# How many steps of a superstep have a fixed place: one instead of two, in a graph network that builds its adjacency matrix by one-hot products

## The reference: what is computed

```python
    def _sage_conv(x, src, dst, W_l, b_l, W_r):
        msg = x[src]
        summed = jax.ops.segment_sum(msg, dst, num_segments=N_NODES)
        cnt = jax.ops.segment_sum(jnp.ones((src.shape[0],), x.dtype), dst, num_segments=N_NODES)
        aggr = summed / jnp.maximum(cnt, 1.0)[:, None]
        return aggr @ W_l + b_l + x @ W_r
...
    for l in range(L):
        agg = jax.ops.segment_sum(h[src], dst, num_segments=N) / deg
...
edge_index = jnp.stack([src, dst])
x = _layernorm(x + _L0_gnn_ref(x, edge_index, ...))
x = _layernorm(x + _L1_gnn_ref(x, edge_index, ...))
```

## Time and profile before

| | |
|---|---|
| median of 3 runs | 2031.82 us (2031.15 to 2037.95) |
| the profiled execution | 2040.89 us, of it 2039.1 us in the span |
| loop that builds A | 92 to 399 us of the span |
| PE, PEld busy over the span | 1772.0 us (87%), 1376.1 us (67%) |
| DVE, ACT, POOL busy over the span | 892.9, 829.7, 619.0 us |
| mean granted clock of TensorE | 0.907 |

### The profile page before, as it was taken

One profiled execution on the slowest core, in us unless ns is written; L12 is line 12 of the kernel. 1 busy time (PEld: TensorE's weight loads), 2 busy tenths in 40 slices (PEclk: granted clock), 3 DMA queues, 4 the chain that ended last, 5 costly groups with the idle time before them and its releaser, 6 DMA issues.

```text
span 2039.1 us, 30707 instructions
## 1 busy us (share of the span) xinstructions
PE 1772.0 (87%) x9747; PEld 1376.1 (67%) x9748; DVE 892.9 (44%) x2593; ACT 829.7 (41%) x1404; POOL 619.0 (30%) x593
## 2 busy tenths in 40 slices
PE   3856666589999998999979998999979998999974
PEld 2545555445566654888868877888868777888864
DVE  6589999834344335533321113433321113433324
ACT  6156666634322222333326563333336663333321
POOL 1044444300000033444430231544430221644430
PEclk9866666689999999999999998999989997999986
DMA  6970000034566783354448551454458541544441
GB/s 145 341 265 0 0 0 0 24 128 173 197 204 222 244 312 123 74 114 74 71 73 283 196 192 44 83 111 72 68 107 284 184 165 43 96 68 74 74 114 51
DMA packets 162537, 259.54 MB, mean 127 GB/s; under 512 B 27776, under 2 KB 136043, under 8 KB 162424
## 3 DMA queue, kind: packets, MB, share of 16 engines
q1 hardware_dynamic: 125960, 206.09, 31.5%
q0 software_dynamic: 36464, 51.98, 14.5%
HBM read 149.08 MB, written 108.94 MB: 127 GB/s over the span
## 4 chain that ended last, share of the span: by engine, by line
PE 76%; DVE 12%; issue 5%; ACT 3%; DMA 2%; DVEq 1%; SPq 1%; POOL 0%; ACTq 0%; POOLq 0%
PE psum L1685 17%; PE psum L1696 16%; PE psum L1507 14%; PE psum L1594 13%; DVE arena L764 7%; PE psum L1651 2%; PE psum L1487 2%; PE psum L1674 2%; PE psum L1422 2%; PE psum L1454 2%; PE psum L1452 1%; PE psum L1645 1%; PE psum L1718 1%; DVEq L764 1%; PE psum L1478 1%
## 5 line engine op out<-in xcount | busy, mean ns | idle before, releaser
L669 POOL DMA_INDIRECT h_rows<-arena,idx x192 | 312.9, 1629 | 420.5 <-DVE arena L1115 374.7
L1359 ACT ACTIVATE arena<-psum,b1c 128x256 f32<-128x256 f32 x384 | 181.8, 473 | 462.5 <-PE psum L1685 462.5
L1685 PE MATMUL psum<-arena 128*128 128x256 f32 x1536 | 360.6, 389 | 6.7 <-ACT arena L1356 6.7
L1696 PE MATMUL psum<-arena 128*128 x1536 | 347.4, 379 | 0.0
L1685 PEld LDWEIGHTS psum<-arena 128*128 128x128 f32 x1536 | 281.1, 193 | 70.9 <-ACT arena L1359 18.7
L1507 PE MATMUL psum<-arena 128*128 128x384 bf16 (+1 forms) x1875 | 316.9, 326 | 0.5 <-ACT arena L1243 0.2
L1696 PEld LDWEIGHTS psum<-arena 128*128 128x128 f32 x1536 | 284.6, 190 | 34.8
L764 DVE TENSOR_TENSOR arena<-arena 125x1200 bf16<-125x1200 bf16 (+1 forms) x300 | 282.4, 1008 | 20.4 <-PE psum L1454 19.5
L1507 PEld LDWEIGHTS psum<-arena 128*128 128x128 bf16 x1875 | 181.5, 98 | 125.7 <-ACT arena L1246 3.2
L644 POOL DMA_INDIRECT xs_d<-arena,pos x150 | 146.3, 976 | 390.4 <-DVEq L946 348.4
L1113 DVE TENSOR_TENSOR arena<-psum,arena 128x256 f32<-128x256 f32 x192 | 80.9, 421 | 378.2 <-PE psum L1696 377.0
(11 more groups left out here) (252 smaller groups left out, 1751.2 us busy)
## 6 DMA issues: line engine op xcount, KB each, us to landing
arena<-adj_d SPq DMA_DIRECT2D x54, 800.0 KB, 4.5
ring<-adj_d SPq DMA_DIRECT2D x46, 800.0 KB, 4.5
xs_d<-zrow SPq DMA_DIRECT2D x8, 3432.0 KB, 27.3
arena<-xs_d SPq DMA_DIRECT2D x96, 264.0 KB, 2.8
adj_d<-arena SPq DMA_DIRECT2D x25, 800.0 KB, 4.4
h_rows<-zrow SPq DMA_DIRECT2D x1, 8192.0 KB, 39.3
h_new<-h_rows SPq DMA_DIRECT2D x12, 640.0 KB, 8.0
arena<-h_rows SPq DMA_DIRECT2D x10, 640.0 KB, 6.7
```

The lines of the kernel that those rows point to most:

```text
L669: pool.indirect_dma_start(h_rows, bass.IndirectOffsetOnAxis(ap=idx[:, j % 2, h:h + 1], axis=0), ybuf[:, j % 2, h], None, compute_op=ALU.ad ...
L1359: act.activation(hid[:, j % 2, f], psum[:, 5 + f % 2, 0:M], ACT.Relu, bias=b1c[:, bass.ds(at_b1[j % LOAD] + f, 1)]).then_inc(b_hidf, 1)
L1685: mm = pe.matmul(psum[:, 5 + f % 2, 0:M], w1s[:, j % 2, f // 2, kt, f % 2 * P:(f % 2 + 1) * P], xsT[:, j % 2, kt], start=(kt == 0), stop=( ...
L1696: mm = pe.matmul(psum[:, h, 0:H], hid[:, j % 2, f, h * P:(h + 1) * P], w1f[:, bass.ds(at_w2 + f * H, H)], start=(f == 0), stop=(f == FT - 1))
```

## The change

NST goes from 2 to 1. Only step z = 0 has a fixed place; step z = 1 gets its place from a register like the other six. So `ohe` holds one step of each superstep with 200 columns (it was two with 300), `oh2` holds seven steps of each (it was six), `w_rel` has seven numbers for a superstep, and the keys are split accordingly. The count of matmuls stays. The diff, whole but for the file's head:

```diff
-NST = 2
+NST = 1
 EC = (NST + 1) * WC
...
         oh2 = carve([NOH, B16 // G * (G - NST) // 2, WC, 2], BF16, CE)
-        ohe = carve([2, B16 // G, EC, 2], BF16, CE)
+        ohe = carve([2, B16 // G // 2, EC, 2], BF16, CE)
...
-            pool.iota(iota_e[:, :, :], [[1, EC], [-WC, 2]], base=-WC, ...).then_inc(s_const, 1)
+            pool.iota(iota_e[:, :, :], [[1, EC], [0, 2]], base=-WC, ...).then_inc(s_const, 1)
...
                             if z < NST:
                                 cols = (z + 2) * WC
-                                pe.matmul(bank[:, 0:cols], oh1[:, q, n, :, z % 2], ohe[:, q % 2, g, 0:cols, z], start=(z == 0), stop=False, skip_group_check=True)
+                                pe.matmul(bank[:, 0:cols], oh1[:, q, n, :, z % 2], ohe[:, q % 2, g // 2, 0:cols, g % 2], start=(z == 0), stop=False, skip_group_check=True)
                                 continue
                             mm = pe.matmul(bank[:, bass.ds(rel[(q % 2 * k + g) * (G - NST) + z - NST], WC)], oh1[:, q, n, :, z % 2],
-                                           oh2[:, q, (g * (G - NST) + z - NST) // 2, :, z % 2], start=False, stop=(z == G - 1), skip_group_check=True)
+                                           oh2[:, q, (g * (G - NST) + z - NST) // 2, :, (g * (G - NST) + z - NST) % 2], start=False, stop=(z == G - 1), skip_group_check=True)
```

More of the change, by code:

```diff
@@ L590, in _ @@
             pool.iota(iota2[:, :, :], [[1, P], [0, 2]], base=0, channel_multiplier=0, allow_small_or_imprecise_dtypes=True).then_inc(s_const, 1)
-            pool.iota(iota_e[:, :, :], [[1, EC], [-WC, 2]], base=-WC, channel_multiplier=0, allow_small_or_imprecise_dtypes=True).then_inc(s_const, 1)
+            pool.iota(iota_e[:, :, :], [[1, EC], [0, 2]], base=-WC, channel_multiplier=0, allow_small_or_imprecise_dtypes=True).then_inc(s_const, 1)
             pool.wait_ge(s_zero, 3)
```

## The result

The changed kernel takes 2071.54 us (median of 4 runs, 2068.98 to 2077.69), the kernel before 2034.88 us (4 runs, 2031.15 to 2040.63). The ratio is 1.0186, with a 95% interval of 1.0154 to 1.0217: 38 us slower by the ratio, 37 by the medians. The forecast was 36.5.

A forecast was written before the change was run, and what follows sets the result against it. TensorE's sequencer was taken to bound the loop: 50 half turns x (0.27 read + 0.44 moved step) = 35.5, plus 1 for early half turns, is 36.5 us; 2031.82 + 36.5 = 2068 us, range 2054 to 2077.

The forecast's parts named there:

- The bound: Loop that builds A: TensorE's sequencer sets the half turn of 5.914 us; VectorE, though 96% busy, follows.
- The register read: L1435 in the loop: 28 registers instead of 24 cost 0.27 us more in each half turn, on the path.
- The moved step: Step z = 1 in every superstep, placed by a register instead of fixed: 0.11 us net, 0.44 us a half turn.
- the bank's wait: Wait instruction in TensorE's superstep: taken as two thirds of the 0.11 us it shares with three fixed pairs.
- The early half turns: First seven half turns, beside the writing of zeros: slow register reads lengthen with the count, taken as 1 us.
- Nothing outside the loop: Before the loop, tables change shape at 0, plus or minus 0.2 us; later stages are shifted and otherwise alike.
- VectorE bounds the loop: Rival in the loop: less compare work makes each batch 0.29 us shorter, 29 us off, 2003 us; chance 0.07.
- The cheap issue: Rival in the loop: added issue costs half or partly falls into slack; 24.5 us slower, 2056 us; chance 0.12.
- The array as the limit: Rival variant in the loop: 200 columns fewer a superstep take 43 us off, 1989 us; within the chance of 0.07.
- The bank's release as the pace: Rival at L1446: TensorE waits for ScalarE's L1206, which absorbs the added issue; about 2032 us, no change; chance 0.03.
- The loop's end: Sign in the profile of the changed kernel: the loop runs from 92 to about 435 us.

The follow-up runs named there:

- e1: Kernel before, with the register read at L1435 taking 28 registers instead of 24, the four more unused: half turn 6.171 us, ratio to before 1.012.
- e3: Kernel before, with VectorE's leading one-hots in the loop 200 columns wide instead of 300: half turn 5.914 us, ratio to before 1.003.
- e4: Changed kernel, with one more VectorE compare of 360 elements in each batch: half turn 6.672 us, ratio to the kernel before 1.017.
- e7: Changed kernel without TensorE's waits for oh1 and oh2, keeping that for ohe: half turn 6.413 us, ratio to the kernel before 1.016.
- e2: Changed kernel, with the register read at L1435 taking 24 registers instead of 28: half turn 6.416 us, ratio to the kernel before 1.014.
- e9: Kernel before, unchanged, run again on chip 10: half turn 5.914 us, first to last read 304.2 us, ratio to before 0.996.
- e10: Changed kernel, run again on chip 10: half turn 6.673 us, first to last read 341.9 us, ratio to the kernel before 1.012.

## Why the prediction was right

*The bound.* Shown. The argument was that the batch's one-hots are ready 2.7 and 1.6 us before they are used. A read that is 0.257 us longer makes the half turn 0.257 longer (e1), 0.20 us less of compare in a batch changes nothing (e3), 0.34 us more changes nothing in the changed kernel (e4), and a wait instruction less in each batch gives back 0.259 us in a half turn there (e7).

*The register read.* Forecast 0.27 us for four registers, measured 0.257: 12.9 of 13.5 us. The slope from ScalarE's 8 to TensorE's 24 registers, 67 ns each, nearly held at 28 (64 ns).

*The moved step.* Taken at 0.11 us for each superstep, with bounds of 0.087 and 0.122; measured 0.126 (e2), just over the upper bound. This is the term that the sum had too small. The address instructions of L1454 start 0.124 us apart (median) in both kernels; so a step placed by a register costs the sequencer about what was measured, and the fixed matmul that it replaces nothing that can be told from it. The two thirds that the prediction gave to the bank's wait were a guess, and the pair's 0.012 us with them. The sum became 50 x 0.502 = 25.1 us instead of 22. The Trainium skill's price for an issued matmul ("TensorE: Matmul & The Clock Gate", section "Wait — 56ns, not 53.3ns?", about 62 ns where hardware decode is off) doesn't fit here: by it the net price would be 0.06 us. The same section says that with hardware decode on a matmul goes to the engine without the sequencer's microcode, and with that the measurement agrees; no run here shows how the decode was set.

*The early half turns.* I took 1 us for reads that are slow beside the writing of zeros. From e9 to e10 the first nine half turns grew by 7.3 us, of which 9 x 0.759 = 6.8 is the plain price; 0.5 us is left. In e1 they grew by 3.7 us against e9, where 9 x 0.257 = 2.3 is the plain price, so 1.4 is left there. The 1 us lies between the two, and two pairs don't settle its size. In the first pair of profiles they grew by 11.7 us, since the kernel before had started late.

*Nothing outside the loop.* Shown for the first pair: behind the last read the two profiles differ by 1.6 us. The loop's growth, 37.7 us (e9, e10), is also close to the difference of the medians in the result, 36.7 (31 to 44 us by the ratio). On chip 10 it is open, as said above. The sum of 36.5 was 1.2 us short of the loop's growth. It had 3.1 us too little for the step; against that stand 0.65 us too much for the read, 0.5 for the early turns, and 0.8 since between the first and the last read lie 49 half turns and not 50. That the forecast agrees with the medians to 0.2 us is luck; by the ratio the difference is 38, and the runs of each kernel spread over 9 us.

*The rivals.* That VectorE bounds the loop was refuted by e1, e3, e4 and e7, though the busy share of 96% and the list of waits both spoke for it. The rule of the Trainium skill ("Perfetto Trace Analysis", section "Identifying the Most-Contended Engine") would have chosen VectorE in the loop; the engine with the most busy time there had 0.2 to 0.4 us of slack in each half turn, and the limit was in instructions that count in no engine's busy time. The cheap issue wanted 6.13 us in e2 and got 6.416. The array as the limit would have gained by 200 columns fewer; e2 has them fewer with the read unchanged, and its half turn is 0.502 us longer. The bank's release as the pace: e1 and e7 show it false, since a longer or a shorter issue would have gone into that wait.

*What I called a sign.* The loop's end was forecast for about 435 us and came at 425.6, because this execution started the loop 15 us earlier. The length of the loop was the better sign: forecast 343 us (92 to 435), measured 348.7 (76.9 to 425.6).

## What to carry to other kernels

Look for the sequencer's own instructions line by line wherever a loop uses registers: reads of many offsets, address computations and waits don't count as busy, and here the list of waits put their time down to VectorE. A wait is to be believed if the awaited instruction ends just before the waiting one starts; here it had ended 2.7 us before. Then change one thing at a time and read the period: it showed 0.257 us where the whole time, with a spread of 40 us, showed little. In this loop it was a loss to take 200 columns from the array and 300 elements from VectorE for each superstep, since neither set the pace, and to give the full sequencer one more address instruction and one more register to read.

## What was not expected of the hardware

- The read of registers from on-chip memory into TensorE's sequencer has hardly a fixed part: 1.617 us for 24 and 1.874 for 28, thus 64 ns for each further register and 67 on average. ScalarE's read of 8 took 0.549 us, 69 ns each. Beside full DMA traffic (share 1.02) single reads took up to 5.8 us with 24 registers (e9) and 6.9 with 28 (e1).
- To turn a matmul with a fixed address into one with a computed address costs the sequencer 0.126 us (e2), the whole spacing of the latter, 0.124.
- TensorE's clock was at its lower level for the whole loop of the changed kernel (0.50), and part of the time in the kernel before (0.64); the period doesn't show it (5.746 us for the short half turns of the kernel before, at the lower level alone or at both).
- The same program in the first pair and on chip 10: half turns of 5.913 and 5.914 us, and 2035 against 2126 us for the whole.
